# Attention and layer norm over 32 batches on one core: two groups of heads turned in squares by VectorE in place of one, a shared PSUM bank, new engine orders, and every batch written out

## The reference

```
q = x @ Wq.T ; k = x @ Wk.T ; v = x @ Wv.T + bv          # per head: 256 x 32
a = q k^T * 384**-0.5 + adj                              # per head: 256 x 256
a = softmax(a)   (rows that are zero throughout give 0)
o = a v          (heads side by side: 256 x 384)
y = layernorm(x + o @ Wo.T + bo)                         # no scale, no shift
```

## Time and profile before

| | us |
|---|---|
| median of 3 runs | 809.9 (808.43 to 810.4) |
| the profiled execution | 806.81 |
| its span, first to last instruction | 805.0 |

### The profile page before, as it was taken

One profiled execution on the slowest core, in us unless ns is written; L12 is line 12 of the kernel. 1 busy time (PEld: TensorE's weight loads), 2 busy tenths in 40 slices (PEclk: granted clock), 3 DMA queues, 4 the chain that ended last, 5 costly groups with the idle time before them and its releaser, 6 DMA issues.

```text
span 805.0 us, 26421 instructions
## 1 busy us (share of the span) xinstructions
PE 769.8 (96%) x7992; PEld 662.7 (82%) x7992; DVE 579.2 (72%) x2184; ACT 632.6 (79%) x2055; POOL 454.5 (56%) x518
## 2 busy tenths in 40 slices
PE   7789999999999999999999999999999999999873
PEld 6677888888888888888888888888888888888652
DVE  2567777777777877777787777778777777877842
ACT  2468888888888888888888888888888888888851
POOL 2535656765565676556567655656765565574322
PEclk7999999999999999999999999999999999999996
DMA  7044453445535344554534455453445545344441
GB/s 234 1 172 171 152 187 126 163 138 189 189 150 188 126 155 142 184 189 150 188 125 156 143 182 189 151 187 132 149 149 177 189 154 184 132 148 138 140 144 39
DMA packets 71072, 124.80 MB, mean 155 GB/s; under 512 B 3712, under 2 KB 50560, under 8 KB 66944
## 3 DMA queue, kind: packets, MB, share of 16 engines
q1 hardware_dynamic: 71040, 124.40, 44.4%
HBM read 78.25 MB, written 46.14 MB: 155 GB/s over the span
## 4 chain that ended last, share of the span: by engine, by line
PE 91%; DMA 3%; DVE 2%; POOL 1%; issue 1%; ACT 1%; SPq 0%; ACTq 0%; POOLq 0%; DVEq 0%
PE bank_b L540 42%; PE t_bank L597 16%; PE bank_a L627 12%; PE s_bank L586 10%; PE t_bank L540 8%; PE t_bank L608 3%; DMA sq_probT<-sq_dram 1%; DMA sq_dram<-w_f 1%; DVE neg L813 1%; DMA w_f<-in_wqT 1%; ACT prob L444 1%; POOL kq_lo L340 0%; DVE y L901 0%; POOL o_lo L350 0%; POOL kq_hi L338 0%
## 5 line engine op out<-in xcount | busy, mean ns | idle before, releaser
L444 ACT ACTIVATE prob<-neg,negmax 128x256 f32<-128x256 f32 x768 | 380.8, 500 | 38.0 <-PE t_bank L597 30.1
L813 DVE CUSTOM_DVE_ANT_0 neg<-s_bank,bias 128x256 f32<-128x256 f32 x512 | 183.7, 420 | 60.5 <-PE s_bank L586 42.2
L597 PE MATMUL t_bank<-ident,prob 128*128 128x128 f32 x1024 | 152.6, 282 | 0.8 <-ACT kq L425 0.5
L597 PEld LDWEIGHTS t_bank<-ident,prob 128*128 128x128 f32 x1024 | 110.2, 141 | 49.2 <-issue 28.4
L444 ACT ACTIVATION_READ_ACCUMULATOR prob<-neg,negmax 128x1 f32 x768 | 146.5, 191 | 0.0
L340 POOL TENSOR_TENSOR kq_lo<-kq,kq_hi 128x512 fp32r<-128x512 f32 x96 | 125.0, 1302 | 7.7
L540 PE MATMUL bank_b<-xt_hi,w_hi 128*128 128x256 f32 x384 | 115.3, 300 | 5.5 <-DVE w_lo L794 2.5
L366 POOL TENSOR_SCALAR var_eps<-meanvar 128x2 f32<-128x2 f32 x32 | 7.3, 228 | 183.0 <-DVE meanvar L911 183.0
L540 PE MATMUL bank_b<-xt_hi,w_lo 128*128 128x256 f32 x384 | 109.9, 286 | 0.0
L540 PE MATMUL bank_b<-xt_lo,w_hi 128*128 128x256 f32 x384 | 109.8, 286 | 0.0
L454 ACT ACTIVATE probT<-t_bank 128x512 f32<-128x512 f32 x160 | 93.7, 586 | 9.7 <-PE t_bank L597 9.6
(11 more groups left out here) (68 smaller groups left out, 1864.7 us busy)
## 6 DMA issues: line engine op xcount, KB each, us to landing
sq_dram<-w_f SPq DMA_DIRECT2D x32, 1024.0 KB, 3.9
sq_probT<-sq_dram SPq DMA_DIRECT2D x32, 1024.0 KB, 5.7
xt<-in_xT SPq DMA_DIRECT2D x32, 384.0 KB, 3.5
xr<-in_x SPq DMA_DIRECT2D x32, 384.0 KB, 6.2
out_y<-y_out SPq DMA_DIRECT2D x32, 384.0 KB, 2.6
bias_sq<-in_adjP SPq DMA_DIRECT2D x32, 256.0 KB, 6.3
bias<-in_adj SPq DMA_DIRECT2D x32, 256.0 KB, 6.3
w_f<-in_wkT SPq DMA_DIRECT2D x3, 192.0 KB, 4.1
```

Source lines behind the costliest of these rows:

```text
L444: nc.scalar.activation(prob[:, u % PROB_RING, k], neg[:, h, w.c], ACT.Exp, scale=-1.0, bias=negmax[t.p][:, w.c, h:h + 1], accum_out=sums[t ...
L597: last = nc.tensor.transpose(t_view[u % 2][:, k, m, :], prob[:, u % PROB_RING, k, P * m:P * (m + 1)], ident[:])
L813: nc.vector.tensor_tensor_reduce(out=neg[:, h, w.c], in0=s_bank[h % JH][:, w.c, :], in1=by[t.p][:, w.c, :], scale=-1.0, scalar=BIG, op0=AL ...
```

## The change

Two groups go in squares (units 0 to 7) in place of one; units 8 to 11 stay on TensorE, and ScalarE copies all four. There is a second staging area, scratch tensor and pair of transfers. The two `t_bank`s become one `bank_t`, and K01, R0 and R1 share a bank of their own, `bank_c`. K01 is saved with one instruction. The loop is gone: `steps` calls `step` for batches -2 to 33, all written out. The orders of all engines are new.

```diff
-SQUARED = 1
+SQUARED = 2
-ON_DVE = (4, 6, 8)
+ON_DVE = ()
...
-def steps(eng, body):
-    for c in range(-2, 4):
-        body(Batch(0, c))
-    with eng.Fori(2, 15) as i:
-        body(Batch(i, 0))
-        body(Batch(i, 1))
-    for c in range(2 * 15, 34):
-        body(Batch(0, c))
+def steps(body):
+    for c in range(-2, 34):
+        body(Batch(c))
...
-    t_bank = [nc.alloc_psum_tensor(f"t_bank{k}", [P, NT * N], F32) for k in range(2)]
-    bank_a, bank_b = (nc.alloc_psum_tensor(f"bank_{x}", [P, NT * N], F32) for x in "ab")
+    bank_t = nc.alloc_psum_tensor("bank_t", [P, PAIR, NT, P], F32)
+    bank_a, bank_b, bank_c = (nc.alloc_psum_tensor(f"bank_{x}", [P, NT * N], F32) for x in "abc")
...
-            "Y0": bank_b, "Y1": bank_b, "K01": t_bank[0], "R0": t_bank[1], "R1": t_bank[1]}
+            "Y0": bank_b, "Y1": bank_b, "K01": bank_c, "R0": bank_c, "R1": bank_c}
...
                 if nxt2.alive and nxt2.c >= 2:
                     load_xt(nxt2)
+                if nxt.alive and not nxt.first:
+                    load_bias(nxt)
                 if t.alive:
                     store_squares(t, 0)
                     load_squares(t, 0)
+                    store_squares(t, 1)
                     load_xr(t)
-                if nxt.alive and not nxt.first:
-                    load_bias(nxt)
+                    load_squares(t, 1)
...
                 if name == "K01":
-                    nc.scalar.activation(kq[:, 0, :].rearrange("p (m b r) -> p m r b", m=NT, b=BLOCKS),
-                                         bank[name][:, 0:N].rearrange("p (m r b) -> p m r b", m=NT, b=BLOCKS), ACT.Copy)
-                    nc.scalar.activation(kq[:, 1, :], bank[name][:, N:2 * N], ACT.Copy).then_inc(kq_saved[name], 1)
+                    nc.scalar.activation(kq[:, 0:2, :].rearrange("p a (m b r) -> p (a m) r b", m=NT, b=BLOCKS),
+                                         bank[name][:].rearrange("p (a m r b) -> p (a m) r b", a=2, m=NT, b=BLOCKS),
+                                         ACT.Copy).then_inc(kq_saved[name], 1)
```

More of the change, by code:

```diff
@@ L50, with __init__ @@
 class Batch:
[L53 to L57, removed]
+    def __init__(self, c):
+        self.c, self.p = c, c % 2
+        self.alive = 0 <= c < B
+        self.first = c == 0
     def count(self, per_batch, extra=0):
-        return self.i * (2 * per_batch) + (self.c * per_batch + extra)
+        return self.c * per_batch + extra
     def later(self, k):
-        return Batch(self.i, self.c + k)
+        return Batch(self.c + k)
     def loads(self):
-        return DMA * (self.c // 2 + 1) + self.i * DMA
+        return DMA * (self.c // 2 + 1)
     def copies(self, u, on_dve):
@@ L302, in step @@
                     store_out(prev2)
-            steps(sp, step)
+            steps(step)
             sp.wait_ge(stored, DMA * B)
@@ L321, in split_xt @@
                 after(pool, v_done, t.count(NT, -NT))
-                if t.c == 1 and not t.looped:
+                if t.c == 1:
                     pool.wait_ge(xt_ready, 1)
@@ L398, in step @@
                 if prev.alive:
+                    split_o_lo(prev, 0)
                     split_o_lo(prev, 1)
-            steps(pool, step)
+            steps(step)
         @block.scalar
@@ L736, in step @@
+                if t.alive:
+                    pe.wait_ge(flag_read, t.count(1, 1))
+                    weigh(t, 0)
+                    copied(t, 9)
+                    transposes(t, 10)
+                if prev.alive:
+                    pe.wait_ge(o_n_ready, prev.count(2, 1))
+                    spread(prev, 1)
                 if nxt.alive:
                     if nxt2.alive:
-                        pe.wait_ge(kq_saved["K2Q0"], nxt2.count(1, 1))
+                        pe.wait_ge(kq_saved["Q12"], nxt2.count(1, 1))
@@ L769, in step @@
-                if t.alive:
-                    pe.wait_ge(o_saved[0], t.count(1, 1))
-                    weigh(t, 1)
-                    copied(t, 8)
-                    transposes(t, 10)
-            steps(pe, step)
+                    scores(nxt, 1)
+            steps(step)
         @block.vector
@@ L917, in step @@
                 if t.alive:
-                    add_bias(t, 2)
-                    save_v(t, 1)
                     add_bias(t, 3)
                     square(t, 0)
+                    save_v(t, 0)
+                    if t.first:
+                        w_lo_part(W_O)
+                    square(t, 1)
+                    add_bias(t, 4)
+                    square(t, 2)
+                    add_bias(t, 5)
+                    save_v(t, 1)
                 if prev.alive:
@@ L932, in step @@
                 if t.alive:
-                    add_bias(t, 7)
-                    square(t, 3)
-                if prev2.alive:
-                    moments(prev2, 0)
-                    residual(prev2, 1)
-                if t.alive:
+                    square(t, 4)
+                    square(t, 5)
                     add_bias(t, 8)
+                    square(t, 6)
+                    square(t, 7)
                     add_bias(t, 9)
@@ L942, in step @@
                     add_bias(t, 11)
+                if prev2.alive:
+                    moments(prev2, 0)
+                if t.alive:
                     find_zero(t)
-                    copy_probT(t, 4)
+                if prev2.alive:
+                    residual(prev2, 1)
+                if t.alive:
                     read_flag(t)
+                    mask(t)
+                if nxt.alive:
+                    add_bias(nxt, 0)
+                if prev2.alive:
+                    moments(prev2, 1)
+                if nxt.alive:
+                    add_bias(nxt, 1)
                 if prev.alive:
                     divide(prev, 0)
-                if prev2.alive:
-                    moments(prev2, 1)
-                if t.alive:
-                    copy_probT(t, 6)
-                    mask(t)
+                if nxt.alive:
+                    add_bias(nxt, 2)
                 if prev.alive:
                     divide(prev, 1)
-                if nxt.alive:
-                    save_v(nxt, 0)
-                    if nxt.first:
-                        w_lo_part(W_O)
-                    add_bias(nxt, 0)
-                if t.alive:
-                    copy_probT(t, 8)
-                if nxt.alive:
-                    add_bias(nxt, 1)
-            steps(dve, step)
+            steps(step)
 _INS = ["x", "xT", "adj", "adjP", "wqT", "wkT", "wvT", "bv", "woT", "bo"]
```

205 lines of the change are left out of this document (88 added, 117 removed).

## The result

The changed kernel takes 780.61 us (median of 4; 778.31 to 782.45) against 809.16 for the kernel before on the same chip: a ratio of 0.967 (95% interval 0.963 to 0.970), 28.6 us faster. Forecast were 754 (56 us faster), 745 to 766 as my own range, and 742 to 790 as the wide one. The sign is right and the wide range holds the time, the narrow one does not: half of the forecast gain is missing.

A forecast was written before the change was run, and what follows sets the result against it. TensorE's list of work was taken as the bound. Span 805.0 - 6.3 (start) - 51.8 (28 periods at 1.85 less) + 1.9 (end) = 748.8; profiled execution 750.6, median of runs 754, own range 745 to 766, wide 742 to 790.

The forecast's parts named there:

- The bound, and what leaves it: TensorE's list of work, 23.45 us a batch, sets the period; 16 transposes less a batch leave it.
- The pieces, 21.6: Sum of TensorE's pieces in a middle batch: 21.6 us, 1.85 less than before, bounds 21.4 to 21.8.
- the three new neighbours: TensorE pairs in no row (weighing to scores, scores to projection twice): each worth 0 to 0.15 us, to either side.
- xt is issued: Load of x on SP, about 1 us before the step, needed by 5.0: 3.5 to land, hidden, 2.5 us to spare.
- the lay-out: Hand-laid times in one step for when each engine's results and transfers are ready and needed; all margins positive, least 0.3 us.
- The transfers are late: Rival: the first weighing waits as group 0's load lands late; 4 us of lateness gives 784 us; chance 0.05.
- Part of the gain goes into new waits: Rival: TensorE waits for flag, second scores or single transposed bank; 0.5 us idle a batch gives 769; chance 0.18.
- The Trainium skill's rule on HBM access under load: With both trips of group 0's squares at high load, the first weighing would wait 0.6 us a batch; not used.
- The other side: Rival: VectorE's 5.6 us idle a batch is hand-over with ScalarE and stays: period 24.2 us, time 832; chance 0.06.
- K01 in one instruction, 0.5 to 1.0: ScalarE's save of that projection by one strided instruction, not two: 0.5 to 1.0 us, taken as 0.75, no change.
- Written out: 0: Leaving the loop and streaming more instructions costs 0 us, bounds -0.1 to +0.3 a batch.
- The tail, 46.6: From the start of step 31 to the end of the span: 46.6 us, kept as in the kernel before.

The follow-up runs named there:

- half of the traffic: Changed kernel with store and load of group 1's squares moving half of the blocks from the second batch on: 762.5 us, ratio 0.945.
- the changed kernel's second profile: The changed kernel itself, unaltered, measured again beside the version with the moments moved, on one chip: 777.8 us, ratio 0.964.
- moments first: Squares' transfers first, x a step ahead, last add_bo late; VectorE's second moments moved between read_flag and mask: 760.4 us, ratio 0.942 against the kernel before.

## Why the prediction was right or wrong

- *The bound, and what leaves it.* Right. TensorE's list set the period before and sets 21.85 of the 22.36 now. The transposes went from 1024 matmuls to 512, and the K01 piece of batch 3 came 7.2 us earlier for the 6.3 that were forecast.
- *The pieces, 21.6.* Too low by 0.25, with the measured 21.85 just above the upper bound of 21.8; 7.0 of the 28.9 us. The mis-sized term is the three new neighbours, "each worth from 0 to 0.15": S2 to K2Q0 and S0 to Q12 cost 0.20 each. The Trainium skill's rule (TensorEngine Tiling (Array Packing), Key Properties) that a change of tiling mode drains the engine has the right direction in these rows, but my use of it, counting changes and so going lower, was wrong: they do not cost the same (W1 to S2 nothing that the rows show).
- *DMA: "xt is issued ... and has until 5.0: with 3.5 to land that is hidden, 2.5 to spare".* This is the step that failed. The issue came where it was laid out, 1 us ahead of the step. The 3.5 was read where the load of squares had landed almost 5 us earlier; now x is issued while the second group's load is in flight, and it became 5.9 at the median and up to 8.1 in the middle. I had asked the question of a fuller queue only for the squares themselves, which the lay-out protected with 3 us, and not for the other five transfers a batch. Halving group 1's traffic took the whole 14.2 us of the periods back. The price stood in the page of the kernel before: a load of the same size that is issued behind a load of squares.

```profile
xr<-in_x SPq DMA_DIRECT2D x32, 384.0 KB, 6.2
```

  With 6.2 in place of 3.5, the lay-out has x landed at 5.2, past its 5.0.
- *The rivals.* "The transfers are late" had 5%, at W0 and for a lateness of 4 us. The mechanism was that one, at K2Q0 and for half of its price. "Part of the gain goes into new waits" named flag, S1 and the transposed bank; in the changed kernel none of them holds up a matmul in the middle, so those margins, though of 0.3 us, were good. That the wide range holds the time is owed to these two rivals, and as neither named the wait that came, it is in good part luck.
- *The Trainium skill's rule on HBM access under load* (DMA: Bandwidth & Descriptors, Latency and other measured facts), 0.2 us on average and 2 us at high load, was set aside because no row showed it. For x and for the output's store the runs agree with its direction: 5.9 for 3.5 and 5.1 for 2.6 us. But xr, issued no longer behind a load of squares, lands in 4.6 for 6.2, and group 0's store in 4.1 for 3.9, although the kernel as a whole has more traffic. What is in flight at the issue counts; the runs do not tell such a latency from mere queueing behind other bytes.
- *The other side*, VectorE and ScalarE bound by handing over: refuted. With half of the traffic VectorE is idle 3.8 us of 21.85 and TensorE never.
- *ScalarE: K01 in one instruction, 0.5 to 1.0.* It took 1,101 ns, more than the upper bound and more than the 0.73 of the two; hidden, since ScalarE has room.
- *Written out: 0.* Right.
- *The tail, 46.6.* 9.3 short in this profile, some 7 in the second. I let the new tail be as long as the old. In the profile it is this chain:

```profile
733.74 0.57 DVE y L870
734.33 6.78 DMA xr<-in_x
...
741.25 0.16 POOL xr L370
...
743.00 1.95 POOL o_lo L344 x2
...
745.09 3.22 PE bank_b L532 x9
748.31 1.91 PE bank_a L619 x16
...
753.19 2.34 PE bank_b L532 x9
...
759.52 0.69 ACT y_out L468
760.21 0.53 ACT o_hi L462
...
760.88 1.95 POOL o_lo L344 x2
```

  and in the kernel before, where Y1 of batch 30 had gone ahead of the last weighing:

```profile
783.28 1.00 PE bank_a L627 x16
...
788.33 1.91 POOL o_lo L350 x2
```

  The last weighing ends 31.4 us after step 31's start (753.19 - 721.8), where it was 25.9 (784.28 - 758.42): 5.5 later. On the way there, Y0 of batch 30 comes 4.5 later than the 18.8 that the lay-out had, and it takes 3.22 us where it takes 1.59 in the middle (granted clock 0.60 from there to the end). From the last weighing to the split of the last o it is then 7.7 us where it was 4.1, since the new order has Y1 of batch 30 and its whole normalisation in between: 3.6 more. The rest is as long as before (16.8 and 16.7). The 3.6 is a consequence of the order on TensorE and ScalarE, read from the chain and tested by no run; the changed kernel's second profile, half of the traffic and moments first have 7.1 or 7.2 there. Of the 5.5, the load of xr may be a part: taking it out of the chain gave 3.4, 1.3 and nothing in three comparisons, with 2.3 between two profiles of one kernel.

## What to carry to other kernels

A time from issue to landing belongs to the traffic in which it was read. When a change adds transfers, go through every DMA of the period, those left alone above all, and see what will be in flight when it is issued; take its landing from a transfer of its size that already has such neighbours (here the 6.2 of xr for the 3.5 of x), and see which has no room; then issue first what is wanted first, and whole steps ahead where the buffer is free. And when the order on TensorE changes, price each new pair of neighbours by shape: the sum over pieces is only as good as the pairs that the old order shows.

## What the hardware showed

- The 384 KB load of x landed in 3.5 us in the kernel before (DMA engines busy 0.47 of the time), 4.7 with half of group 1's traffic (0.66), and 5.9 in the changed kernel (0.76), by medians; in the kernels with x issued elsewhere or further ahead, 7.1 to 7.9 at 0.76 to 0.78. The mean share alone does not set it: xr, of the same size, landed in 6.2 at 0.47, behind a load of squares, and in 4.6 at 0.76.
- Reading one register from SBUF on VectorE's sequencer took 0.30 us with four loads in flight and the DMA engines full (0.99), and 1.22 at the median with a store, x, a bias and xr in flight. Which of these makes it long is open.
- A copy from PSUM of 512 elements with strides took 1,101 ns in one instruction, 598 contiguous.
- A projection of 18 matmuls took 2.15 us behind another projection, 2.35 behind scores or a weighing.
